# Attention with the pieces of P in fixed PSUM banks, and a table of indices in 16 bits

## What is computed

```python
h = jnp.maximum(_layernorm(x, axis=-1), 0.0)
x = x + _L1_gnn_ref(h, src, dst, ...)
# in _L1_gnn_ref: 8 heads of 64
e = jnp.einsum('ehd,ehd->eh', k[src], q[dst]) / np.sqrt(DK).astype(np.float32)
m = jax.ops.segment_max(e, dst, num_segments=n)
ex = jnp.exp(e - m[dst])
z = jax.ops.segment_sum(ex, dst, num_segments=n)
attn = ex / z[dst]
a = jax.ops.segment_sum(attn[:, :, None] * v[src], dst, num_segments=n)
```

## Time and profile before

| what | us |
|---|---|
| median of 3 runs | 1135.5 |
| the three runs | 1133.88, 1135.5, 1138.69 |
| span of the profiled execution (first to last instruction) | 1133.4 |
| the fastest run, which is the nearest to it | 1133.88 |
| attention, 40 units | 449 to 768 |
| count stage | 50 to 217 |

### The profile page before, as it was taken

How to read it: one execution, slowest core, us unless ns; L and a number is a source line. 1 busy time by engine, 2 the same in 40 slices (tenths; PEclk the granted TensorE clock), 3 DMA queues, 4 the chain that set the end, 5 groups by cost and what they waited for, 6 DMA issues and landing times.

```text
span 1133.4 us, 16827 instructions
## 1 busy us (share of the span) xinstructions
PE 1052.5 (93%) x5904; PEld 689.2 (61%) x5904; DVE 583.0 (51%) x1743; ACT 445.4 (39%) x762; POOL 157.7 (14%) x182
## 2 busy tenths in 40 slices
PE   6988878899999999899999999999899998999998
PEld 3456656555444554677777777774456896555443
DVE  7888998610884011666665666655447337300133
ACT  6502565400645101565555656552436415410000
POOL 0000000000053000333333000005537012000000
PEclk9999998899999999999999999999999999999999
DMA  5003788850100000554544100026001051100010
GB/s 169 1 0 106 221 259 269 261 178 1 40 35 1 19 19 31 177 152 150 152 140 144 42 1 1 2 82 245 0 1 47 1 192 36 38 1 1 10 46 35
DMA packets 73097, 93.63 MB, mean 83 GB/s; under 512 B 7169, under 2 KB 63176, under 8 KB 73022
## 3 DMA queue, kind: packets, MB, share of 16 engines
q1 hardware_dynamic: 73022, 92.62, 26.1%
HBM read 58.00 MB, written 34.60 MB: 82 GB/s over the span
## 4 chain that ended last, share of the span: by engine, by line
PE 79%; DVE 10%; issue 5%; ACT 4%; DMA 1%; SPq 1%; DVEq 0%; ACTq 0%
PE PS L557 8%; PE PS L788 8%; PE PS L590 8%; PE PS L771 8%; PE PS L936 7%; PE PS L743 7%; PE PS L971 6%; PE PS L714 5%; PE PS L613 5%; PE PS L529 2%; DVE R L1241 2%; PE PS L700 2%; DVE HT L1106 2%; PE PS L891 2%; PE PS L918 2%
## 5 line engine op out<-in xcount | busy, mean ns | idle before, releaser
L557 PE MATMUL PS<-HT,R 125*128 125x313 bf16 x636 | 130.5, 351 | 27.0 <-DVE HT L1106 15.8
L1230 DVE CUSTOM_DVE_ANT_0 HT<-PS,CD 128x1250 f32<-128x1250 f32 (+1 forms) x80 | 116.4, 1455 | 67.4 <-issue 67.4
L557 PEld LDWEIGHTS PS<-HT,R 125*128 x636 | 98.0, 172 | 59.9 <-issue 45.4
L771 PE MATMUL PS<-K,HT 128*128 128x128 f32 (+2 forms) x800 | 112.5, 280 | 15.0 <-DVE R L1241 14.4
L1535 ACT COPY R<-PS 128x512 f32<-128x512 f32 (+1 forms) x120 | 64.8, 574 | 121.5 <-PE PS L771 119.5
L1555 ACT ACTIVATE HT<-HT,soft 128x1250 f32<-128x1250 f32 (+1 forms) x80 | 107.1, 1338 | 10.3 <-DVE soft L1233 3.3
L771 PEld LDWEIGHTS PS<-K,HT 128*128 128x128 f32 (+2 forms) x800 | 84.0, 140 | 43.2 <-DVE R L1241 23.6
L743 PE MATMUL PS<-R 64*128 64x512 f32 (+3 forms) x480 | 95.8, 531 | 3.1 <-DVE soft L1230 3.1
L788 PE MATMUL PS<-R 128*64 128x128 f32 (+2 forms) x1600 | 94.2, 273 | 0.0
L788 PEld LDWEIGHTS PS<-R 128*64 128x64 f32 (+1 forms) x1600 | 84.8, 137 | 6.4 <-issue 5.8
L590 PE MATMUL PS<-CD,H 128*128 128x512 f32 (+2 forms) x240 | 86.0, 520 | 2.4 <-ACT X L1445 2.4
(11 more groups left out here) (222 smaller groups left out, 1386.2 us busy)
## 6 DMA issues: line engine op xcount, KB each, us to landing
edge_parts<-X SPq DMA_DIRECT2D x160, 156.5 KB, 2.7
R<-edge_parts SPq DMA_DIRECT2D x60, 156.5 KB, 2.3
CD<-edge_sums SPq DMA_DIRECT2D x1, 6250.0 KB, 20.8
CD<-edge_parts SPq DMA_DIRECT2D x10, 469.5 KB, 3.8
BC<-edge_parts SPq DMA_DIRECT2D x30, 156.5 KB, 2.5
CD<-edge_parts SPq DMA_DIRECT2D x3, 1565.0 KB, 10.8
edge_sums<-R SPq DMA_DIRECT2D x20, 156.5 KB, 2.8
R<-edge_parts SPq DMA_DIRECT2D x18, 155.5 KB, 2.3
```

Source lines behind the costliest of these rows:

```text
L557: return mm(bank(b0 + h, QUART), stat, hot, start=first, stop=True, skip_group_check=True)
L771: m = nc.tensor.transpose(PS[0:rows(j), o:o + n], Pb[u % 2][a][0:n, j * P:j * P + rows(j)], ident[0:n, 0:n])
L1230: ve.tensor_tensor_reduce(Pb[s][a][0:n], PS[0:n, a * N:(a + 1) * N], cd[0:n, t, :], 1.0, -3e38, ALU.add, ALU.max, soft[0:n, s, a:a + 1]).t ...
```

## The change

**1. Banks.** Each piece gets a fixed bank by its number in the unit, `PIECE_BANK = (6, 7, 6, 7, 4)`. Piece 4 goes to bank 4, the last bank of the scores. The waits follow: piece 2 waits for the copy of piece 0, piece 3 for that of piece 1, piece 0 of the next unit for that of piece 2, piece 1 for that of piece 3. Piece 4 waits instead for the maxima of the next unit (`s_max` at 2u + 4), since DVE reads the next unit's scores from bank 4. And the third pair of products of `scores(u)`, which writes bank 4 again, waits for the copy of piece 4 of unit u-2.

**2. The table.** `winI` holds 16-bit unsigned numbers instead of 32-bit ones. As the numbers can be negative, 16384 is added on DVE when the table is made and taken off again in the registers: in `fixed_chunk` within a constant that was there already, in `late_chunk` by one more addition.

```diff
+SHIFT = 16384
+PIECE_BANK = (6, 7, 6, 7, 4)
-        winI = BC[0:1, 1200:1200 + NG * VALUES].bitcast(I32)
+        winI = BC[0:1, 1200:1200 + NG * VALUES].bitcast(U16)[:, 0:NG * VALUES]
...
         def fixed_chunk(d, m, q):
-            return bass.ds((d + m + (q - FIX)).with_bounds(min_val=q, max_val=NC - FIX - 1 + q), 1)
+            return bass.ds((d + m + (q - FIX - SHIFT)).with_bounds(min_val=q, max_val=NC - FIX - 1 + q), 1)
         def late_chunk(d, m):
-            return bass.ds((d + m).with_bounds(min_val=FIX, max_val=NC - 1), 1)
+            return bass.ds((d + m + -SHIFT).with_bounds(min_val=FIX, max_val=NC - 1), 1)
...
                         if (j, a) == (2, 0):
                             pe.wait_ge(sem("s_half"), u + 1)
+                            if u >= 2:
+                                piece_out(PIECES * (u - 1) - 1)
...
                 if i == 0:
                     pe.wait_ge(sem("p_exp"), 2 * u + 2)
-                if c >= 2:
+                if i >= 2 and i < 4:
                     piece_out(c - 2)
+                elif i < 2 and u > 0:
+                    piece_out(c - PIECES + 2)
+                elif i == 4 and u + 1 < UNITS:
+                    pe.wait_ge(sem("s_max"), 2 * u + 4)
                 for jj in range(2):
                     j = 2 * i + jj
                     for a in range(2):
-                        o = (6 + c % 2) * BANK + (2 * jj + a) * P
+                        o = PIECE_BANK[i] * BANK + (2 * jj + a) * P
...
-                    link(ve.tensor_scalar(ends, ends, 1.0 - FIX, None, ALU.add))
+                    link(ve.tensor_scalar(ends, ends, 1.0 - FIX - SHIFT, None, ALU.add))
```

More of the change, by code:

```diff
@@ L22 @@
 I32 = mybir.dt.int32
+U16 = mybir.dt.uint16
 P = 128
@@ L1241, in _ @@
                         ve.tensor_copy(PT[c % RING].rearrange("p (j n) -> p j n", j=4)[:, :, 0:n],
-                                       bank(6 + c % 2).rearrange("p (j n) -> p j n", j=4)[:, :, 0:n])\
+                                       bank(PIECE_BANK[i]).rearrange("p (j n) -> p j n", j=4)[:, :, 0:n])\
                             .then_inc(sem("pt_dve"), 1)
@@ L1535, in piece @@
                 sc.copy(PT[c % RING].rearrange("p (j n) -> p j n", j=4)[:, :, 0:n],
-                        bank(6 + c % 2).rearrange("p (j n) -> p j n", j=4)[:, :, 0:n]).then_inc(sem("pt_act"), 1)
+                        bank(PIECE_BANK[i]).rearrange("p (j n) -> p j n", j=4)[:, :, 0:n]).then_inc(sem("pt_act"), 1)
             def spread(v):
```

## The result

The changed kernel is slower: 1163.7 us as a median of four runs, 1162.6 to 1165.4, beside 1136.9 for the kernel before. The ratio is 1.0265, with an interval from 1.0236 to 1.0293. Forecast were 1112.8 us and a gain. The profiled execution took 1164.5 us, with a span of 1162.5.

What follows compares the result with a forecast made beforehand. PE, busy 93% of the span, was taken as the bound, idling in attention mainly for DVE's copies. 1135.5 - 22.7 (banks) + 0 (table) = 1112.8 us, range 1106.5 to 1118.

Steps and rivals of the forecast that it cites:

- The attention part: Attention: with the new banks PE no longer waits for DVE's copies before piece 4; 22.7 us less, range 21 to 23.5.
- Rivals 3, 4 and 5: In attention: wait only halved, 1124, chance 0.08; piece 4 released no sooner, 1135, 0.04; fifth product waits for DVE, 1154, 0.03.
- The register program: Count stage: one more addition in `late_chunk`, taken as 10 ns a step, 1 to 2 us more in sum.
- The load of 20 numbers: Count stage: the ten table loads on PE get about 0.55 us shorter each; 2.5 of them count, 1.4 us less.
- The rule of the Trainium skill: Table loads: about 200 ns a register even in bulk, so half the width would save nothing.
- What PE gains or loses after 131 is thus taken up by SP: Late count stage: SP, 12.19 us per four groups against PE's 10.97, is slower, so seven of ten loads don't count.
- Rival 2: Count stage: SP does not end it, nine loads count, 2 to 7 us saved, middle 5, so 1107.8; chance 0.12.
- The rival on the side of a loss: Attention: the scores' fifth product waits 1.0 us a unit for DVE's late copy of piece 4, 1154 us; chance 0.03.
- the part that I had costed at nothing: The table's effect on the count stage, loads and register program together: sum 0, between -2.5 and +2.5 us.

Runs made afterwards that it cites:

- the banks alone: Kernel before with only the new piece banks, 32-bit table without offset, and a mask on each loop's end that changes no value: 1111.8 us, ratio 0.9808.
- the kernel with the offset alone: Kernel before with the 16384 offset and longer register program, but a 32-bit table, old banks and a mask on each loop's end: 1136.9 us, ratio 1.0022.
- The run that loads twice: Kernel with only the new banks, 32-bit table, in which both engines load the same 20 numbers twice for every four groups: 1133.3 us.

## Why the prediction was wrong

**The attention part was right, to the size.** The sum had 22.7 us less; the banks alone measured 22.8 less, and their whole time, 1111.8, lies 1 us from the forecast of 1112.8. Its steps held too: twelve transposes in one row, and a copy of piece 4 that ends 0.4 us before the ninth weight load, where the prediction had put it at 0.4. Rivals 3, 4 and 5 fall.

**The register program was right.** I took 10 ns a step and had 1 to 2 us. DVE's row went from 55 to 67 ns, and the kernel with the offset alone came out 2 us longer, with an interval from 0.7 to 4.4.

**The step that failed is the term "The load of 20 numbers".** It was bounded from half saved to 0.3 us more a load, and taken as 0.55 less. Measured are 5.3 us more a load by the medians, 5.2 by the sums. Two things were wrong in it. The trace had no load of another width, and I closed the bound on the side of a loss with the sentence that no row spoke for clumsy narrow reads. But no row spoke against them either: the only row for the operation was of one width and one start, so it could not bound what a change of both would do. And I read 70 to 137 ns a number as a price of the number. It was a quarter of a fetch of 0.26 to 0.53 us, cheap only because the 32-bit table is 32-bit and its loads start 80 bytes apart. The spread of 1.39 to 2.73 does go with memory traffic: the loads at 51.9 and 102.9 us, with a DMA share of 0.00 and 0.46, took 1.55 and 1.39, the later ones, at 0.68 to 0.95, 1.96 to 2.73. But it says nothing of how reads are cut, though I took it to.

The rule of the Trainium skill, "Runtime: NRT & Kernel Launch", section "Instruction fetch mechanics", was set aside in the prediction since the trace had it cheaper. An estimate by it is 20 x 0.2 = 4.0 us a load, which is 1.3 to 2.6 more than the rows, or 13 to 26 us over ten loads. It gives both kernels the same 4.0, so it forecasts no loss either; but the gap was a sign that something in the kernel before made its loads cheap, and that this could be lost.

**A second step failed beside it: "What PE gains or loses after 131 is thus taken up by SP".** With it even a loss of 5.3 a load would have come out as 2.5 x 5.3 + 7 x (10.97 + 5.3 - 12.19) = 42, not 52, so this was the smaller error. PE's 10.97 us for four groups was one round. PE's last six rounds in the trace before, from load to load, average 11.3, and SP's fetches lag behind at 12.19 as the buffers fill up; a queue that lags is not yet one that holds up. The run that loads twice made the late rounds longer by the whole of its second load, 11.5 to 13.5 us. Rival 2 named this mechanism, but with the sign of the term above. None of these runs makes the loads clearly cheaper than in the kernel before with the short register program, so whether SP would hold up a faster PE stays open.

The rival on the side of a loss was placed in attention, where I had measured most, at 0.03. The loss came from the part that I had costed at nothing.

## What to carry to other kernels

Before the width, the packing or the address of something that is read into registers is changed, price that load by its own small run: here it was a sequencer's stop of 2 us, and a change that halves its bytes, or moves them by four, made it 7.6. Keep register tables 32-bit, start every load at a multiple of 16 bytes and load a multiple of four words, padding where need be. An operation of which the trace shows only one form has no bound on the other side; give it a range that is wide on both sides, and a chance of its own.

The better version here is the banks alone with the table left as it was (it has the mask too): 1111.8 us, 0.9808 of the kernel before and some 52 us under the changed one.

## What the chip showed that I had not expected

- A load of registers took about 0.1 us and 0.21 to 0.25 us a fetch with a DMA share of 0.00, and 0.37 to 0.43 a fetch amid the copies of the windows (7487 ns for twenty fetches; 1959 and, as the median of the earlier trace rows, 2263 for five). Four aligned words cost one fetch; a 16-bit number cost one as well, whatever its start.
- The number of words is no measure of the time: 354 ns for four, 743 for three; 1359 for twenty, 1795 for nineteen.
- The granted clock of TensorE in the stretch from 131 to 217 us was 0.77 in the changed kernel and 0.88 before, a mix of its levels of 1.2 and 2.4 GHz. In the changed kernel it fell to the lower one during each of PE's loads from the second on (104.3 us), while PE had little to do for 6 to 9 us, and rose again behind it. The products of the count stage lasted 364 ns on average in place of 351. What the clock costs by itself no run shows: from the banks alone to the table moved by one word the stage grows by 1 us less than its loads.
